# A graph layer's edge loop and its last phase: a leftover tile every 12 blocks in place of 15, and the loads of the last phase issued earlier

## The reference

```python
pre_u = jnp.einsum('bud,dk->buk', h_t, W1[:d])
pre_v = jnp.einsum('bvd,dk->bvk', h_t, W1[d:])
hidden = jax.nn.relu(pre_u[:, :, None, :] + pre_v[:, None, :, :] + b1)
S = jax.nn.sigmoid(jnp.einsum('buvk,ko->buvo', hidden, W2)[..., 0] + b2[0])
a_t = jnp.einsum('buv,bud->bvd', S * A_a, h_t)
m_t = jnp.einsum('uv,bud->bvd', A_m, h_t) * h_t
z_t = beta1 * h_t + beta2 * (jnp.einsum('bvd,de->bve', a_t, Wa) + ba) + beta3 * (jnp.einsum('bvd,de->bve', m_t, Wm) + bm)
```

## Time and profile before

| what | value |
|---|---|
| median of 3 runs | 3439.96 us (3439.62 to 3442.63) |
| the profiled execution: its time, its span | 3444.2 us, 3442.2 us |
| TensorE busy | 3354.5 us, 97% of the span |
| VectorE busy | 2837.3 us, 82% |
| ScalarE busy | 2338.0 us, 68% |
| GpSimd busy | 1833.4 us, 53% |
| the chain that ended last | TensorE 58%, VectorE 8%, issue 2%, DMA 1% |

### The profile page before, as it was taken

The page is one execution under the profiler, slowest core; times in us unless marked ns, Lnnn a source line. Parts: engine busy times, 40 slices in busy tenths (PEclk is TensorE's granted clock), DMA queues, the critical chain, the costliest instruction groups (busy, mean ns, idle before and its releaser), DMA issues.

```text
span 3442.2 us, 56132 instructions
## 1 busy us (share of the span) xinstructions
PE 3354.5 (97%) x14230; PEld 2617.6 (76%) x14230; DVE 2837.3 (82%) x4857; ACT 2338.0 (68%) x14070; POOL 1833.4 (53%) x2379
## 2 busy tenths in 40 slices
PE   7999999999998999999999999999999999789999
PEld 5667667676666888788878888878878888678888
DVE  5566765766546999999999999999999999569897
ACT  1212121211116999899999999999999999788997
POOL 3222222221115667656666666666765665678886
PEclk9999999999998999999999999999999999999999
DMA  7876776767669557765675766676757657587775
GB/s 271 296 260 240 264 259 243 283 248 255 234 205 233 138 122 177 166 161 125 156 169 128 177 142 167 159 165 140 183 132 169 148 114 186 202 288 251 263 258 191
DMA packets 345403, 685.81 MB, mean 199 GB/s; under 512 B 38990, under 2 KB 252856, under 8 KB 323512
## 3 DMA queue, kind: packets, MB, share of 16 engines
q1 hardware_dynamic: 289088, 594.50, 59.9%
q0 software_dynamic: 21504, 53.31, 5.0%
q10 hardware_dynamic: 34480, 34.34, 2.9%
HBM read 444.01 MB, written 256.18 MB: 203 GB/s over the span
## 4 chain that ended last, share of the span: by engine, by line
PE 58%; DVE 8%; issue 2%; POOL 1%; DMA 1%; ACT 0%; SPq 0%; POOLq 0%
PE psum_d L1313 15%; PE psum_d L1314 15%; PE z_psum L1610 11%; PE psum_a L1313 9%; PE psum_a L1314 9%; DVE group_sum L1355 4%; DVE late_sum L1352 1%; DVE mixed L1359 1%; DMA shared<-sum_dram 1%; DVE left_mixed L1359 1%; DVE group_sum L1380 1%; DVE left_sum L1355 1%; POOL shared L1572 0%; POOL masked L1572 0%; ACT shared L1634 0%
## 5 line engine op out<-in xcount | busy, mean ns | idle before, releaser
L1411 ACT ACTIVATE junk<-psum_a 128x128 f32<-128x128 f32 x6144 | 1606.7, 292 | 205.8 <-PE psum_a L1314 112.8
L1411 ACT ACTIVATION_READ_ACCUMULATOR junk<-psum_a 128x1 f32 x6144 | 1366.1, 223 | 0.0
L1355 DVE TENSOR_REDUCE group_sum<-psum_d 128x56 f32<-128x896 f32 x1024 | 1112.2, 1086 | 90.6 <-PE psum_d L1314 47.3
L1314 PE MATMUL psum_d<-v_t,pk 128*128 128x512 f32 x1920 | 753.4, 392 | 0.0
L1463 POOL DMA_INDIRECT sum_dram<-total,idx_all x512 | 505.9, 988 | 228.0 <-POOL total L1474 124.1
L997 POOL TENSOR_TENSOR own<-whole 128x256 f32<-128x256 f32 x128 | 125.9, 983 | 754.3 <-DVE own_mixed L789 420.5
L1313 PE MATMUL psum_d<-u_t,pk 128*128 128x512 f32 x1280 | 503.0, 393 | 3.8 <-issue 2.8
L687 PE MATMUL wide<-shared,h 128*128 128x512 f32 x1024 | 482.2, 593 | 0.0
L746 ACT COPY whole<-ring 128x256 f32<-128x256 f32 x128 | 47.6, 372 | 630.5 <-PE ring L659 630.5
L1314 PE MATMUL psum_a<-v_t,pk 128*128 128x512 f32 x1152 | 452.7, 393 | 0.0
L1314 PEld LDWEIGHTS psum_d<-v_t,pk 128*128 128x128 f32 x1920 | 360.8, 188 | 79.9
(11 more groups left out here) (234 smaller groups left out, 6256.9 us busy)
## 6 DMA issues: line engine op xcount, KB each, us to landing
rows_dram<-split SPq DMA_DIRECT2D x128, 512.0 KB, 3.2
sum_dram<-zero SPq DMA_DIRECT2D x128, 512.0 KB, 4.1
u_t<-rows_dram SPq DMA_DIRECT2D x64, 1024.0 KB
shared<-sum_dram SPq DMA_DIRECT2D x64, 1024.0 KB, 6.2
first_u<-rows_dram SPq DMA_DIRECT2D x62, 1024.0 KB
pk<-pick_dram SPq DMA_DIRECT2D x448, 128.0 KB
whole_dram<-whole SPq DMA_DIRECT2D x128, 256.0 KB, 3.4
pick_dram<-first_v SPq DMA_DIRECT2D x128, 256.0 KB, 3.0
```

The costliest lines, as they stand in the source:

```text
L1314: return nc.tensor.matmul(dst, pk[n % PKS][:, SLOTS + at:SLOTS + at + P], part(v_t[jj][:], b, LB), start=False, stop=True)
L1355: nc.vector.tensor_reduce(out_[:, :, 1:EG], in_[:, :, GW:LATE].rearrange("p b (g k) -> p b g k", k=GW), AX, ALU.add, apply_absolute_value= ...
L1411: last = nc.scalar.activation(junk[:, a % RING_A, k * LATE:(k + 1) * LATE], psum_a[a % RING_A][:, k * LATE:(k + 1) * LATE], ACT.Abs, accum ...
```

## The change

`SPAN` becomes 12, so the last leftover tile is scattered in block 203 and `AHEAD` becomes 204. In the 52 blocks left, GpSimd adds the raw sums of three gate tiles (k = 0, 1, 2), half a tile in every fourth block from 212 to 232. SyncE loads raw tiles 2 and 3 in the loop (blocks 220 and 228), the `hWa` tiles 1, 2 and 3 in blocks 252, 253 and 255, where the u and v tiles whose place they take are no longer read, and tile 4 and raw tile 4 right behind the loop. The wait for the last scatter now stands behind these loads. To make this possible the tiles in SBUF are laid out in another order. ScalarE loads the first tile `z` after k = 1 in place of k = 5. The core of the diff:

```diff
         shared = sb("shared", [P, 3 * ROW])
+        rows_scope = ctx.enter_context(ExitStack())
+        first_u = sb("first_u", [P, ROW], fp32r, scope=rows_scope)
+        first_v = sb("first_v", [P, ROW], fp32r, scope=rows_scope)
         work = ctx.enter_context(ExitStack())
+
         ident = sb("ident", [P, P], scope=work)
         left_base = sb("left_base", [P, LEFT], scope=work)
+        left_tmp = sb("left_tmp", [P, 3, LEFT], scope=work)
         ones_col = sb("ones_col", [P, 1], scope=work)
+        own_sign = sb("own_sign", [P, NG], scope=work)
...
-        SPAN = n_blk // (LEFT + 1)
+
+        SPAN = 12
+        assert SPAN * (LEFT + 1) <= n_blk
         QUARTER = ROW // 4
         RAW = 2
-        AHEAD = n_blk - 8
+        AHEAD = SPAN * (LEFT + 1)
+        HALF_AT = [AHEAD + 8 + 4 * i for i in range(6)]
+        assert HALF_AT[-1] < n_blk - VG
         assert all(n < AHEAD - 8 for n, (s_, j_) in enumerate(blocks) if s_ < 4 and j_ < 2)
...
+
+            def edges_scattered(eng):
+
+                for i in range(RING_S):
+                    eng.wait_ge(scattered[i], 16 * TILES * ((n_blk - i + RING_S - 1) // RING_S))
+                eng.wait_ge(left_scattered, 16 * LEFT)
+
+            def load_hidden(sp, t):
+                sp.dma_start(hWa_all[t], hWa_dram[:, t * P:(t + 1) * P, :].rearrange("b p d -> p b d")).then_inc(hWa_loaded[t], 16)
+
+            def load_raw(sp, k):
+                vt, t = divmod(k, NT)
+                sp.dma_start(raw[k % RAW], sum_uv[t * P:(t + 1) * P, vt * P:(vt + 1) * P, :]).then_inc(raw_loaded[k % RAW], 16)
...
                         load_u(n // VG + 1)
-                    if n == n_blk - 2 * VG:
+                    if n == AHEAD:
                         sp.dma_start(of_u[:], linear_dram[0, :, :].rearrange("(t p) b -> p t b", p=P)).then_inc(of_u_loaded, 16)
                         for i in range(2):
                             load_of_v(sp, i, of_v[:, i * HV:(i + 1) * HV, :])
-                        sp.wait_ge(left_scattered, 16 * (LEFT - 2))
+                        sp.wait_ge(left_scattered, 16 * LEFT)
...
                             sp.dma_start(adj_first[t][:], adj[t * P:(t + 1) * P, 0:P]).then_inc(adj_loaded[t], 16)
                         sp.dma_start(hWa_ahead, hWa_dram[:, 0:P, :].rearrange("b p d -> p b d")).then_inc(hWa_loaded[0], 16)
-                for i in range(RING_S):
-                    sp.wait_ge(scattered[i], 16 * TILES * ((n_blk - i + RING_S - 1) // RING_S))
-                sp.wait_ge(left_scattered, 16 * LEFT)
+                    if n == HALF_AT[2]:
+                        sp.wait_ge(raw_added, 2)
+                        load_raw(sp, 2)
+                    if n == HALF_AT[4]:
+                        sp.wait_ge(raw_added, 4)
+                        load_raw(sp, 3)
+                    if n == n_blk - VG:
+                        load_hidden(sp, 1)
+                    if n == n_blk - VG + 1:
+                        load_hidden(sp, 2)
+                    if n == n_blk - 1:
+                        load_hidden(sp, 3)
+                sp.wait_ge(filled_d, ND * n_blk)
+                sp.wait_ge(filled_a, NA * n_blk)
+                load_hidden(sp, 4)
+                sp.wait_ge(raw_added, 6)
+                load_raw(sp, 4)
+                edges_scattered(sp)
...
                         scatter(total[slot][:, t, :], idx_all[:, t, col:col + 1], scattered[slot])
-                    if n >= n_blk - 5 and n < n_blk - 1:
-                        k, m = divmod(n - (n_blk - 5), 2)
+                    if n in HALF_AT:
+                        k, m = divmod(HALF_AT.index(n), 2)
                         some = slice(m * HV, (m + 1) * HV)
-                        pool.wait_ge(raw_loaded[k], 16)
+                        pool.wait_ge(raw_loaded[k % RAW], 16 * (k // RAW + 1))
                         pool.wait_ge(of_v_loaded[m], 16)
                         pool.wait_ge(left_d, LD * LEFT)
                         pool.wait_ge(left_a, LA * LEFT)
-                        TT(masked_ahead[k][:, :, some].rearrange("p b v -> p v b"), raw[k][:, some, :], of_v[:, some, :],
+                        TT(masked[k][:, :, some].rearrange("p b v -> p v b"), raw[k % RAW][:, some, :], of_v[:, some, :],
                            ALU.add).then_inc(raw_added, 1)
-                for i in range(RING_S):
-                    pool.wait_ge(scattered[i], 16 * TILES * ((n_blk - i + RING_S - 1) // RING_S))
-
...
         work.close()
+        rows_scope.close()
...
-            hWa_all = [hWa_ahead, *[sb(f"hWa_all{t}", [P, B, D], scope=phase)[:] for t in range(1, NT)]]
+            def hidden(t):
+                return sb(f"hWa_all{t}", [P, B, D], scope=phase)[:]
+
+            hWa_all = [hWa_ahead, hidden(1), hidden(2)]
+            masked = [*masked_ahead, sb("masked2", [P, B, P], scope=phase)[:]]
+            adj_b = [*adj_first, *[sb(f"adj_b{i}", [P, P], scope=phase) for i in range(2, ADJ)]]
             of_vs = [of_v[:, 0:HV, :], of_v[:, HV:P, :], sb("of_v_next", [P, HV, B], scope=phase)[:]]
-            adj_b = [*adj_first, *[sb(f"adj_b{i}", [P, P], scope=phase) for i in range(2, ADJ)]]
-            masked = [*masked_ahead, *[sb(f"masked{i}", [P, B, P], scope=phase)[:] for i in range(2, GM)]]
+            masked.append(sb("masked3", [P, B, P], scope=phase)[:])
+            hWa_all += [hidden(t) for t in range(3, NT)]
...
                         if t == 1 and vt:
                             sp.wait_ge(raw_added, 2 * (k - RAW) + 1)
                             load_of_v(sp, 2 * vt + 1, of_vs[(2 * vt + 1) % 3])
-                        if k >= RAW:
+                        if k >= 5:
...
-                        if k >= RAW:
-                            sp.dma_start(raw[k % RAW], sum_uv[t * P:(t + 1) * P, vt * P:(vt + 1) * P, :]).then_inc(raw_loaded[k % RAW], 16)
+                        if k >= 5:
+                            load_raw(sp, k)
                         if k >= 2:
                             waits(sp, gate_masked, MASKS * (k - ADJ + 1))
                             sp.dma_start(adj_b[k % ADJ][:], adj[t * P:(t + 1) * P, vt * P:(vt + 1) * P]).then_inc(adj_loaded[k % ADJ], 16)
-                        if 1 <= k < NT:
-                            sp.dma_start(hWa_all[t], hWa_dram[:, t * P:(t + 1) * P, :].rearrange("b p d -> p b d")).then_inc(hWa_loaded[t], 16)
+                        if 5 <= k < NT:
+                            load_hidden(sp, t)
...
                         k = vt * NT + t
-                        if k < RAW:
+                        if k < 3:
                             continue
...
                         if t == 2 and vt:
                             store(vt - 1)
-                        if t == 5:
+                        if t == (5 if vt else 1):
+                            if vt == 0:
+                                edges_scattered(act)
                             load_base(vt)
```

More of the change, by code:

```diff
@@ L99, in gnn_edges_kernel @@
         ones = sb("ones", [1, P], scope=work)
-        group_sign = sb("group_sign", [P, EG], scope=work)
-        mixed_sign = sb("mixed_sign", [P, GW], scope=work)
-        own_sign = sb("own_sign", [P, NG], scope=work)
         slot_row = sb("slot_row", [P, SLOTS], scope=work)
         slot_next = sb("slot_next", [P, SLOTS], scope=work)
-        idx_all = sb("idx_all", [P, TILES, NBLK], i32, scope=work)
-        left_u = sb("left_u", [P, LEFT], i32, scope=work)
-        left_v = sb("left_v", [P, LEFT], i32, scope=work)
-        left_at = sb("left_at", [P, LEFT], i32, scope=work)
         restart = sb("restart", [P, N], scope=work)
@@ L114, in gnn_edges_kernel @@
         left_base = sb("left_base", [P, LEFT], scope=work)
+        left_tmp = sb("left_tmp", [P, 3, LEFT], scope=work)
         ones_col = sb("ones_col", [P, 1], scope=work)
+        own_sign = sb("own_sign", [P, NG], scope=work)
+        group_sign = sb("group_sign", [P, EG], scope=work)
+        mixed_sign = sb("mixed_sign", [P, GW], scope=work)
+        idx_all = sb("idx_all", [P, TILES, NBLK], i32, scope=work)
+        left_u = sb("left_u", [P, LEFT], i32, scope=work)
+        left_v = sb("left_v", [P, LEFT], i32, scope=work)
+        left_at = sb("left_at", [P, LEFT], i32, scope=work)
         places = sb("places", [P, 2 * SLOTS], fp32r, scope=work)
-        first_u = sb("first_u", [P, ROW], fp32r, scope=work)
-        first_v = sb("first_v", [P, ROW], fp32r, scope=work)
         loaded = sem("loaded")
@@ L135, in left_indices @@
             link(STT(out=out_at, in0=u_, scalar=float(N), in1=v_, op0=ALU.mult, op1=ALU.add))
-        left_tmp = sb("left_tmp", [P, 3, LEFT], scope=work)
         with ExitStack() as phase:
@@ L1229, in gnn_edges_kernel @@
         with ExitStack() as phase:
+            v_t = [first_v, *[sb(f"v_t{i}", [P, ROW], fp32r, scope=phase) for i in range(1, VG)]]
             u_t = [first_u, sb("u_t1", [P, ROW], fp32r, scope=phase)]
-            v_t = [first_v, *[sb(f"v_t{i}", [P, ROW], fp32r, scope=phase) for i in range(1, VG)]]
```

## The result

The changed kernel takes 3421.73 us (3421.01 to 3423.33, 4 runs); beside it the kernel before took 3440.53 (3439.62 to 3442.63, 4 runs). The ratio is 0.9941, with a 95% interval of 0.9929 to 0.9954: faster by 0.6%, 18.8 us on the medians. The forecast was 3407.5, with a range of 3402 to 3419, so the result lies outside it. The profiled executions differ by more: 3444.2 before, 3421.4 after, 22.8 us.

The account below looks back on a forecast made before the run. The prediction took the last phase as TensorE-bound, with a 32.7 us hole before it from late transfers. Terms -32.7, -3.8 and +4.0 made -32.5 us, taking the median 3439.96 to 3407.5 us; range 3402 to 3419.

Parts of the forecast that it names:

- The last phase: Phase after the edge loop: no feeder of TensorE is late, so the whole 32.7 us come back.
- the hole: TensorE's passage from edge loop to last phase, 2926 to 3098 us in the kernel before; said to cost 32.7 us.
- TensorE, which begins at 2961.7 as before: Start of the last phase: tile k = 0 starts unchanged, since first sigmoid and mask hang on the loop's end alone.
- So a wait of about 4 us: Block 209: TensorE waits for a v tile queued behind block 204's loads; +4.0 us in the sum.
- the batch: SyncE's loads from block 204 (u tile, `of_u`, `of_v`, raw tiles, `adj`, first `hWa`), transfers taken to end 27.6 us later.
- the batch of block 248: The same loads in the kernel before: begun at about 2895.7, transfers ending at 2923.3, 27.6 us later.
- Blocks 51 and 52: Loop: TensorE's waits of 2.00 and 1.83 us go, as a leftover gather moves behind both tiles; gain 3.8 us.
- the sum: Last phase -32.7, blocks 51 and 52 -3.8, block 209 +4.0: -32.5 us in all.
- Blocks 157 to 162: Loop: a gather two blocks ahead of a v tile arises at 157 and 159; nothing in sum, up to 2 us in range.
- The batch in block 204 costs more: Rival: block 209's v tile comes 10 us later still, raw and `hWa` moving at 200 GB/s; net -22, 3417; chance 0.16.
- The last scatter lands late: Rival: loop's end, completion waits for `hWa` and raw transfers, VectorE late by up to 3 us; +5, 3412.5; chance 0.14.

Follow-up runs that it names:

- e6: Changed kernel with `hWa` tiles 1 to 4 and raw tile 4 put back behind the wait for the last scatter: 3441.22 us.
- e1: Changed kernel with GpSimd's addition for k = 3 waiting until both masks of k = 0 are done: 3419.13 us.
- e2: Changed kernel with `hWa` tile 4 and raw tile 4 issued behind the wait for the last scatter, GpSimd's addition left in place: 3424.62 us.
- e3: Changed kernel with block 204's batch of loads issued in block 207, behind the v tile of block 209: 3416.98 us.
- e8: Changed kernel with only the first `hWa` tile of block 204's batch issued in block 207, behind block 209's v tile: 3415.49 us.
- e4: Changed kernel with the first `hWa` tile issued ahead of the wait for the leftovers' last scatter, still in block 204: 3421.66 us.
- e9: Changed kernel with only `of_u` and `of_v` of block 204's batch issued in block 207: 3424.6 us.
- e7: Kernel before the change with `SPAN = 12` and nothing else of the change: 3436.09 us.

## Why the prediction was wrong

*The last phase* was right from its first tile on. No tile after k = 0 waited, k = 10 came 70.7 us after k = 0 (70.5 forecast), and with that 32.4 of the 32.7 us in the hole came back. e6 shows that the gain is lost with the loads behind the scatter; how much of it hangs on the `hWa` tiles and how much on the sums made ready and on the place of `adj` is not shown.

*The step that failed in mechanism* is "TensorE, which begins at 2961.7 as before (ScalarE's first sigmoid at 2956.97 and VectorE's first mask at 2960.25 hang on the loop's end alone)". I checked each feeder for being late and none for being in the way. Moving the additions ahead and taking the wait for the scatters off GpSimd lets its addition for k = 3 begin at 2965.62, right beside VectorE's first mask, which stands still behind it. That costs 4.84 us, and e1 and e2 show the cause. Before, GpSimd waited for a raw tile until 2977.45, long after the first masks. The prediction's own times had a collision in them. It put this addition between 2962 and 2967, and before the change VectorE's second mask stood there:

```profile
2963.26 1.23 DVE L1592 TENSOR_TENSOR shared<-shared,adj_first 128x1024 f32<-128x1024 f32 x1 [1.71 <-ACT shared L1634]
```

The overlap was given no price.

The Trainium skill, GPSIMD Engine Reference, Specifications, says that GpSimd shares its SBUF interfaces with VectorE, in contention with VectorE instructions that have two SBUF inputs. The mask is one, and e1 and e2 agree; the page has no size for it, the runs have: the whole of the addition.

*The term that was mis-sized* is "So a wait of about 4 us" in block 209. The place and the cause were right (e3, e8), the block lost 8.7 us. Of the difference of 4.7 us, 2.3 are the tile's arrival, 43.0 us after the batch began and not 40.7. The trace's records of landings place them. The second half of the v tile arrives in 16 parts: 14 of them were in by 2609.96, 40.8 us after the batch began, the last at 2612.15, and TensorE begins at 2612.21. I had counted the batch of block 248 to the moment when the engines' mean share fell, 2923.3; there too the last part came later, at 2924.8 (2905.84 and 19.0). The new wait for the last two leftover tiles, which I did not work out, makes SyncE issue the first `hWa` tile 16.6 us after the batch began (2585.82 less 2569.2) and not 10.1, but costs nothing here, since the engines are busy with `of_v` until then (e4); e9 shows that it holds the batch up when `of_v` doesn't. The rounding of 4.4 to 4 and the five blocks, which took 36.05 us and not 36.3, make 0.7. And 1.8 us are the clock, which fell to 0.50 in a pause of 7 us; I had priced the pause and not the restart.

*Blocks 51 and 52* were right in place and cause, and e7 shows them with the span alone, but mis-sized too: -3.8 in the sum, -1.2 in the loop as a whole, since waits that end are not blocks that shorten by as much, and since other blocks with leftover work grew. Blocks 157 to 162 showed no wait for a tile.

*The reference time.* The sum was made against a profiled execution of 3444.2 us and taken off the median of 3439.96. The two profiled executions differ by 22.9 us of span, and VectorE's last sums and TensorE's tiles place them: block 209 +8.7, loop's end to k = 0 +4.8, k = 0 to k = 10 -32.4, the other blocks from 9 on -1.2, blocks 1 to 8 -2.4, the rest -0.4. The change does not touch blocks 1 to 8, and in the other runs with the same code there (e1 to e6, e8, e9) they take 79.7 to 82.6 us, against 79.2 here: they vary from execution to execution. That 3411.7 with the two terms above makes 3421.2, and the profiled execution took 3421.4, is therefore luck in part, since the 2.6 us missing in the loop's other blocks and these 2.4 cancel. On the medians all three terms make 3419.6 us (3407.5 + 4.8 + 4.7 + 2.6) and the changed kernel took 3421.73; what makes the other 2.1 us is open.

*The rivals.* "The batch in block 204 costs more" did not come true as it was meant: the raw and `hWa` tiles moved at 378 to 421 GB/s in 2584 to 2597 and not at 200. The 4.7 us more came in the way told above. "The last scatter lands late" came true in its first half: SyncE passed the wait at 2970.14, 4.5 us after the end of GpSimd's last issue (1.3 before the change), and nobody missed it, since ScalarE was the later. Range and chances were too sure of a start time that nothing in the sum had tested.

## What to carry to other kernels

When work is moved forward, ask of each engine not only whether it will be late but what it will now run beside: an idle GpSimd that waited for a transfer was what let VectorE go at full speed. A bulk load put into a queue shared with just-in-time tiles is priced by the next tile behind it, in its place in that queue and up to its last part, and a pause of several us on TensorE costs its restart too. Both losses were undone by moving an issue by three blocks and one addition by 4 us, and that brought nearly what the change had promised.

## What the runs showed of the hardware that was not expected

When GpSimd's two-input addition begins 0.4 us after VectorE's two-input mask, the mask stands still for both halves of the addition, 4.67 us, and ends 1.1 us later; GpSimd is not slowed (in the changed kernel, e2 and e3 alike). When the mask begins during the addition (e1), it waits for one half only: it takes 1.59 us, and the addition 5.66 in place of 4.67. A later mask of the changed kernel, which began at 2980.57, 0.16 us after GpSimd's addition, took 3.29 us and ended 1.1 us after the first half. Why VectorE gets its turn between two GpSimd instructions in one case and not in the other is open; it wasn't tried.

A 2 MB transfer taken out of the queue brought the v tile forward by at least 7 us, where its bytes at 389 GB/s make 5.4 (e8). A transfer's last parts can land 2 us behind the others: of the 16 parts of the v tile's second half in the changed kernel, 14 landed from 2609.50 to 2609.96 and two at 2611.88 and 2612.15.
